# First mixture of experts: the shift of the next group is computed ahead of routing, routing reads its logits in PSUM, and tokens are weighed for two experts at once

## What is computed

```python
x = x + jnp.tanh(g_ffn[0]) * _L0_ffn_ref(_layernorm(x, axis=-1), L0_ffn_gate_w, L0_ffn_We)

def _L0_ffn_ref(x, gate_w, We):
    top_k = 2
    logits = jnp.einsum('btd,ed->bte', x, gate_w)
    top_val, top_idx = jax.lax.top_k(logits, top_k)
    top_w = jax.nn.softmax(top_val, axis=-1)
    y_all = jnp.einsum('btd,edm->btem', x, We)
    x_experts = jnp.take_along_axis(y_all, top_idx[..., None], axis=2)
    out = jnp.sum(x_experts * top_w[..., None], axis=2)
    return out
```

## Time and profile before

| | |
|---|---|
| median of 3 runs | 2269.8 us |
| lowest and highest | 2269.4 and 2273.78 us |
| the profiled execution | 2268.44 us |
| its span, first to last instruction | 2266.7 us |
| instructions | 48312 |
| PE busy | 1969.5 us (87%) |
| DVE busy | 1731.4 us (76%) |
| ACT busy | 1219.1 us (54%) |
| POOL busy | 262.7 us (12%) |
| first instruction of the stage `experts0` (L709) | 671.77 us from the span's start |
| last one (L960 of the last group) | ends at 848.8 us |

### The profile page before, as it was taken

How to read it: one execution, slowest core, us unless ns; L and a number is a source line. 1 busy time by engine, 2 the same in 40 slices (tenths; PEclk the granted TensorE clock), 3 DMA queues, 4 the chain that set the end, 5 groups by cost and what they waited for, 6 DMA issues and landing times. The chain is left out here.

```text
span 2266.7 us, 48312 instructions
## 1 busy us (share of the span) xinstructions
PE 1969.5 (87%) x18173; PEld 1512.4 (67%) x18173; DVE 1731.4 (76%) x4753; ACT 1219.1 (54%) x2340; POOL 262.7 (12%) x553
## 2 busy tenths in 40 slices
PE   3999999999987999999989896999999994699517
PEld 3787888878767987777757574677777773344217
DVE  2888888888867978999957796667666588787886
ACT  2555555555552217888856463445444355209647
POOL 0111111111101102111111142000000022100000
PEclk9999999999997999999989897999999997799759
DMA  6122221112214541111100011221122110003532
GB/s 184 47 51 50 51 50 47 48 48 51 50 28 188 226 188 33 32 30 33 30 4 1 10 57 47 89 99 76 75 100 88 47 48 20 1 0 123 189 133 75
DMA packets 123592, 155.71 MB, mean 69 GB/s; under 512 B 47562, under 2 KB 104291, under 8 KB 119267
## 3 DMA queue, kind: packets, MB, share of 16 engines
q1 hardware_dynamic: 117368, 149.92, 20.4%
q10 hardware_dynamic: 5994, 2.70, 0.4%
HBM read 110.11 MB, written 25.69 MB: 60 GB/s over the span
## 5 line engine op out<-in xcount | busy, mean ns | idle before, releaser
L1717 DVE TENSOR_TENSOR arena<-arena 128x512 f32<-128x512 f32 (+1 forms) x256 | 170.8, 685 | 68.9 <-ACT arena L1755 64.7
L1755 ACT ACTIVATE arena<-banks,b1c 128x512 f32<-128x512 f32 x192 | 131.7, 687 | 170.4 <-PE banks L1630 170.2
L1640 PEld LDWEIGHTS banks<-w2a,arena 128*128 128x128 f32 x1024 | 124.1, 192 | 28.7 <-issue 28.7
L885 PE MATMUL banks<-we,arena 128*128 128x128 f32 x1024 | 130.2, 282 | 3.2
L885 PEld LDWEIGHTS banks<-we,arena 128*128 128x128 f32 x1024 | 121.1, 194 | 10.1 <-DVE arena L949 9.8
L498 PE MATMUL banks<-arena,wk 128*128 128x128 f32 x1024 | 126.8, 278 | 1.1 <-DVE arena L606 1.1
L539 PE MATMUL banks<-wv,arena 128*128 128x512 f32 x256 | 125.1, 611 | 2.6 <-ACT arena L652 2.6
L1640 PE MATMUL banks<-w2a,arena 128*128 128x128 f32 x1024 | 124.7, 275 | 0.0
L498 PEld LDWEIGHTS banks<-arena,wk 128*128 128x128 f32 x1024 | 121.0, 194 | 1.7 <-DVE arena L606 1.5
L1630 PE MATMUL banks<-arena,w1s 128*128 128x512 f32 x256 | 122.0, 611 | 0.0
L633 ACT ACTIVATE arena<-banks 128x512 f32<-128x512 f32 x64 | 38.2, 597 | 143.6 <-PE banks L490 143.6
(11 more groups left out here) (271 smaller groups left out, 5110.2 us busy)
## 6 DMA issues: line engine op xcount, KB each, us to landing
arena<-coef_scratch SPq DMA_DIRECT2D x32, 2048.0 KB, 7.1
arena<-arena SPq DMA_DIRECT2D x256, 64.0 KB, 2.0
gated_scratch<-arena SPq DMA_DIRECT2D x16, 768.0 KB, 3.2
arena<-gated_scratch SPq DMA_DIRECT2D x16, 768.0 KB, 4.3
arena<-z1T_scratch SPq DMA_DIRECT2D x128, 64.0 KB, 2.3
arena<-ctxT_scratch SPq DMA_DIRECT2D x32, 256.0 KB, 2.8
arena<-in_ctx SPq DMA_DIRECT2D x64, 64.0 KB, 2.0
z1T_scratch<-arena SPq DMA_DIRECT2D x64, 64.0 KB, 1.7
```

The lines of the kernel that those rows point to most:

```text
L885: mm = pe.matmul(ps[:, OUT + g.par, j * D:(j + 1) * D], xs[g.par][:, n, j * P:(j + 1) * P], k.we0[:, n, :], start=n == 0, stop=n == EXPERT ...
L1640: mm = pe.matmul(ps[:, OUT + g.par, j * D:(j + 1) * D], hT[g.par][:, c, j * P:(j + 1) * P], w, start=c == 0, stop=c == CHUNKS2 - 1)
L1717: dve.tensor_tensor(hT[g.par][rows, c, :], hT[g.par][rows, c, :], wide_coef[g.par][rows, e, :], ALU.mult).then_inc(s["scaled"].sem, 1)
L1755: act.activation(hT[g.par][:, c, :], ps[:, HID + c % NHID, :], ACT.Gelu, bias=k.b1c[:, c:c + 1])\
```

## The change

Three things change in `vector`, and what follows from them in `tensor`:

- the shift of group s+4 is computed before the routing of group s+3 instead of behind it;
- the routing reads the logits where the matmul left them, in PSUM, and the copy L923 with its semaphore is gone; PE now waits until the routing of the group before has finished before it writes new logits;
- one instruction weighs two experts (128x1024 instead of 128x512), four a group instead of eight; the coefficients are computed behind four weighed experts, not three; and PE waits for each pair.

```diff
+    route.score = ps[:, 1, 0:GROUP * EXPERTS].rearrange("p (j e) -> p j e", j=GROUP)
...
-    s = k.sigs(G, dict(shift=1, l_psum=1, l_sb=1, gap=1, share=2, part=1, coef=1, ct_psum=1, ct_sb=1, scaled=EXPERTS,
+    DUOS = EXPERTS // DUO
+    s = k.sigs(G, dict(shift=1, l_psum=1, gap=1, share=2, part=1, coef=1, ct_psum=1, ct_sb=1, scaled=DUOS,
...
-                if j == 0:
-                    pe.wait_ge(*s["scaled"](g, n + 1))
+                if j == 0 and n % DUO == 0:
+                    pe.wait_ge(*s["scaled"](g, n // DUO + 1))
...
-                    pe.wait_ge(*s["l_sb"](g.back(1)))
+                    pe.wait_ge(*route.done(g.back(1)))
...
-            dve.tensor_copy(route.score, ps[:, LOGITS, 0:COLS].rearrange("p (j e) -> p j e", j=GROUP))\
-                .then_inc(s["l_sb"].sem, 1)
-            dve.wait_ge(*s["l_sb"](g))
             k.hold(dve)
             route.run(dve, g)
...
-            for n in range(first, last):
-                dve.tensor_tensor(by_tile(xs[g.par][:, n]), by_tile(xT[g.idx % LIVE]), spread[g.par][:, n], ALU.mult)\
-                    .then_inc(s["scaled"].sem, 1)
+            wide = [P, DUO, GROUP, P]
+            for n in range(first, last, DUO):
+                dve.tensor_tensor(xs[g.par][:, n:n + DUO].rearrange("p e (j n) -> p e j n", j=GROUP),
+                                  by_tile(xT[g.idx % LIVE]).unsqueeze(1).broadcast_to(wide),
+                                  spread[g.par][:, n:n + DUO], ALU.mult).then_inc(s["scaled"].sem, 1)
...
-            if far:
-                top_two(far)
             if new:
                 dve.wait_ge(*f["rstd_ready"](sub(new, GROUP - 1)))
                 if new.has(1):
                     dve.wait_ge(*f["xhat_ready"](sub(new.back(1), GROUP - 1)))
                 dve.scalar_tensor_tensor(out=shift, in0=k.mv[:, :, 0, 0], scalar=-1.0, in1=k.rstd[:, :, 0],
                                          op0=ALU.mult, op1=ALU.mult).then_inc(s["shift"].sem, 1)
+            if far:
+                top_two(far)
             if nxt:
-                weigh(nxt, 0, 3)
+                weigh(nxt, 0, 4)
             if far:
                 coefficients(far)
             if nxt:
-                weigh(nxt, 3, EXPERTS)
+                weigh(nxt, 4, EXPERTS)
```

## The result

The changed kernel takes 2273.68 us (median of 20 runs), the one before 2268.38 in the same comparison; the ratio is 1.0025, 95% interval 1.0017 to 1.0034. The profiled execution took 2273.16 us, its span is 2271.4.

A forecast was written before the change was run, and what follows sets the result against it. DVE's queue was taken as the bound, the chain through DMA right behind. Full steps +3.0 us, start and end -0.1: +2.9 on the profiled 2268.44, 2271.3; the median 1.36 above, 2272.7 us. Range 2270.2 to 2277.5.

The forecast's parts named there:

- Case A: DVE idles about 1 us for rstd each full step, regaining two thirds elsewhere: 2271 to 2275.5 us; the forecast, chance 0.74.
- Where rstd hides: On DVE, the early shift waits for POOL's rstd: starts 2.96 us into the step, after 1.02 us idle.
- Nothing reads the shift earlier: ACT, the shift's only reader, has the shares and their wait for L929 first, so nothing starts earlier.
- MAX8 behind the shift: On DVE, MAX8 follows the shift by about 0.08 us, at 3.04 instead of 2.27: +0.77 us a step.
- Reads in PSUM: Four MAX8 and four FIND_INDEX8 on DVE read PSUM at no extra cost: taken as 0 a step.
- Pairs: Weighing two experts per DVE instruction saves four fixed parts of 71 ns: -0.28 us a step.
- a full step: DVE's step: 0.69 - 0.28 = +0.41 us, so 9.20 becomes 9.61.
- Stalls: DVE's waits on DMA over eleven full steps mostly vanish: 1.1 us kept of 2.6.
- Start and end: Outside the full steps: 0.7 us saved in steps -3 to -1, +0.6 in step 0; with the end, together -0.1.
- B: Rival, slower: PSUM reads at L692 and L696 have a fixed price, +7.6 us, 2280.3; chance 0.09.
- C: Rival, slower: the wide product suffers from its repeated four-dimensional operand, 10%, +6.8 us, 2279.5; chance 0.06.
- D: Rival, faster or no change: rstd's wait costs little, the chain through DMA becomes the bound, 2269.0 or 2264.9; chance 0.11.

The follow-up runs named there:

- no eps: The changed kernel with POOL's addition of eps to the variance (L735) left out in this stage alone: 2269.79 us, ratio 1.0007 to the kernel before.
- statistics ahead: The changed kernel with a group's statistics and aggregation moved ahead of the second half of the previous step's weighing: 2275.08 us, ratio 1.0033 to the kernel before.

## Why the prediction was right

The forecast was 2272.7 us, with 0.59 for a time within 0.2% of before; it came to 2273.68, in the range, with the difference at the edge of that bound. Case A is what happened: the mechanism was right and its size too small. The change was forecast as +2.9 us and measured as 5.3 (medians) to 5.7 (ratio). That the two totals are only 1.0 us apart is in part luck, since the forecast was added to a median of 2269.8 us for the kernel before, which took 2268.38 in the comparison. Step by step:

- **Where rstd hides.** Right. The shift at 2.96 us is where the sum put it, idle 0.93 instead of 1.02, and with 0.35 us less of POOL ahead of it (no eps) it came 0.36 us earlier.
- **Nothing reads the shift earlier.** Right: ACT's normalising is 0.89 us later in the step.
- **MAX8 behind the shift.** 0.15 us, not 0.08. The copy in the kernel with the shift alone follows the shift by 0.08; MAX8 has the increment of `k.hold` ahead of it, which the sum had left out and which may be why. With PSUM alone the same increment stands between L958 and MAX8, and MAX8 starts 0.64 us behind L958, where the copy stood 0.63 behind L960; so if it costs anything, then behind a short instruction. No kernel without it was tried. +0.07 a step.
- **Reads in PSUM.** Taken as 0, they are 4 to 5 ns each, and with 1.65 us from MAX8 to the difference instead of 1.61 they cost 0.04 a step, within the 0.06 allowed. By the letter this is one of the signs of being wrong that the prediction named (longer than 1.61 us), but it is 0.4 us of the eleven steps. The half microsecond of the Trainium skill's table ("VectorE: DVE Perf Modes", the errata section) did not show on these operations, and following its advice to copy first costs a step of DVE 0.29 us here (9.20 against 8.91 with PSUM alone).
- **Pairs.** 1.219 us each (median), 4.91 us from the first weighed pair to the next statistics: 4.89 was the sum.
- **So a full step** was 9.74 where 9.61 was forecast.
- **Stalls.** The term that was most mis-sized. 1.1 us were kept of 2.6; the changed kernel's full steps hold 110.58 - 11 x 9.74 = 3.4. One step stalled 1.57 us on DMA, and two waited 0.59 and 0.69 us for PE's logits after stretches with the clock at 1.2 GHz (until 713.5 us, and from 758 to 764.8), of which the forecast knew nothing. Idle times before L949 in the full steps were to be fewer and shorter: there was one instead of three, but it lasts as long as the three together (1.57 and 1.61 us).
- **Start and end** were to give -0.1 together and took +0.4 and +1.4. Ahead of step 0 the stage took 0.28 us less, where 0.7 was forecast (the first load was waited for 1.53 us and not 0.96), and step 0 grew by 0.72, not 0.6; the end grew because the loads for groups 14 and 15 were waited for 2.79 and 2.87 us, against 2.5 and 1.5 before.

Rivals B and C fell with the rows of PSUM and of pairs. Of D, the chain through DMA as the limit of a faster DVE, the mechanism is true, though not for this kernel: it is the main reason why PSUM and pairs together, which take 0.57 us off a step of DVE, left the full steps no shorter (105.21 us against 103.83) until the store was issued 2 us sooner. The late clock is the other: with single experts for group 0 they took 101.41 us, 2.4 less than before, where 6.3 would be the whole saving.

Added up by the runs, the parts give 0.36 - 0.16 - 0.09 = +0.11%, and the change +0.25%, within the intervals of the parts, each about 0.14%. The savings by PSUM and by pairs need not add up in any case, since the same chain cuts off both.

## What to carry to other kernels

An instruction moved ahead in an in-order queue takes its wait along, and all that stands behind it then waits too: look at when its input is ready, and at what its reader waits for beside it, before moving it. If an engine is the bound with a chain of transfers close behind, shortening the engine gives little (the full steps averaged 9.44 us before, and 9.45 with DVE's own step 0.29 us shorter), and the cheap move is one that starts the chain sooner: here one copy on ACT, taken out from behind a wait it had no need of, with the other two parts of the change, gave 0.5%, and the same copy alone 0.23%. When an edit is made to take a wait away, see what arrives next: the statistics moved ahead of the weighing met a slower POOL and the logits.

## What was not expected of the hardware

- POOL's operations on a few elements were slowed by DVE's products of two SBUF operands: `var_eps` 0.98 us instead of 0.20, `rstd` 1.80 instead of 1.01, in the kernel with the statistics ahead. In the changed kernel they run beside the added output, which reads PSUM, and an idle DVE, and last 0.20 and 1.01. The Trainium skill has a rule for it ("SBUF — State Buffer", SBUF: two separate sides): a DVE instruction with two SBUF inputs and a GpSimd operation that reads SBUF exclude each other. The trace agrees in its times, though no run tried it by itself: L735 ends at 766.22, and the first of the two L949, started at 764.97 and 1.22 us long, at 766.19.
- The level of TensorE's clock at the start of the stage went with a pause in its first 16 records (0.27 or 0.28 us, once 1.55) in five profiles of six: 1.2 GHz until 712.4 to 713.7 us, where it was left between 701 and 707 us in the other nine, and, in the four with the short pause, 7.4 to 8.1 us instead of 5.52 for the next 48 records.
- The load of 2 MB of spread coefficients takes about 7 us, but in the changed kernel the one issued at 744.36 us, 2.25 us behind its store at 742.11, was used only at 752.91, 8.5 us later, which cost the step 1.57 us. What lengthens single transfers was not tried.
